# One-hot rows of a token behind one another, by twelve narrow compares per tile in place of three wide interleaved operations

## The reference, cut to what matters

```python
xn = _layernorm(x, axis=-1)
s = _L0_attn_ref(xn, ...)
g = _silu(_L0_ffn_ref(xn, ...))
x = x + s * g
# in _L0_ffn_ref: six of 32 experts for each token
idx, w = _route(xf, Wr, br)
gate = jnp.zeros((T, E), w.dtype).at[jnp.arange(T)[:, None], idx].add(w)
h = jnp.square(jax.nn.relu(xf @ w1.T)) @ w2.T      # per expert, acc += g * h
```

## Time and profile before

| | us |
|---|---|
| time, median of 3 runs | 384.15 |
| lowest and highest | 383.17, 384.49 |
| span of the profiled execution, first to last instruction | 381.1 |
| busy: TensorE, VectorE, ScalarE, GpSimd | 308.8, 269.4, 240.6, 221.0 |

### The profile page before, as it was taken

The page is one execution under the profiler, slowest core; times in us unless marked ns, Lnnn a source line. Parts: engine busy times, 40 slices in busy tenths (PEclk is TensorE's granted clock), DMA queues, the critical chain, the costliest instruction groups (busy, mean ns, idle before and its releaser), DMA issues.

```text
span 381.1 us, 8188 instructions
## 1 busy us (share of the span) xinstructions
PE 308.8 (81%) x2716; PEld 234.7 (62%) x2716; DVE 269.4 (71%) x634; ACT 240.6 (63%) x383; POOL 221.0 (58%) x232
## 2 busy tenths in 40 slices
PE   0585886899996878789798888789797798799962
PEld 0353654667785757677575676676475477687841
DVE  4688889998955286647567564447855786699866
ACT  5878799555484676676686576796645653544432
POOL 1966889855877356454663646500076565666750
PEclk9998699899999899999999999999999899899997
DMA  7951160254773366364644646434597565567742
GB/s 262 400 177 58 21 214 24 87 169 137 241 253 101 95 171 206 113 193 126 193 140 132 205 131 211 143 113 136 180 320 223 151 181 150 174 168 207 204 110 83
DMA packets 38762, 62.89 MB, mean 165 GB/s; under 512 B 5026, under 2 KB 26690, under 8 KB 38722
## 3 DMA queue, kind: packets, MB, share of 16 engines
q1 hardware_dynamic: 31474, 42.57, 34.4%
q0 software_dynamic: 7248, 19.80, 18.2%
HBM read 46.66 MB, written 15.70 MB: 164 GB/s over the span
## 4 chain that ended last, share of the span: by engine, by line
PE 52%; DVE 16%; issue 9%; ACT 9%; DVEq 6%; another core or an unknown queue 3%; POOL 2%; ACTq 2%; DMA 1%
PE hp L947 5%; PE hp L945 4%; PE hp L946 4%; PE rot L909 4%; PE hp L932 4%; PE dp L1001 4%; PE dp L1004 4%; PE dp L1003 4%; DVE xs L1284 3%; DVEq L1286 3%; PE hp L934 3%; PE bp L892 3%; DVE hf L1260 2%; PE rot L960 2%
## 5 line engine op out<-in xcount | busy, mean ns | idle before, releaser
L607 POOL DMA_INDIRECT xgt<-xtab,ids x91 | 93.7, 1029 | 63.7 <-PE rot L909 36.3
L617 POOL DMA_INDIRECT wst<-ytab,slot x60 | 62.7, 1045 | 61.3 <-DMA ytab<-wst 27.1
L688 ACT ACTIVATE hf<-hf 128x512 f32<-128x512 f32 (+1 forms) x80 | 49.9, 623 | 72.1 <-DVE hf L1260 52.8
L1001 PE MATMUL dp<-wt,hhi 128*128 128x256 f16 x204 | 56.7, 278 | 5.2 <-ACT xs L722 2.9
L1277 DVE COPY wst<-rot 128x512 f32<-128x512 f32 (+1 forms) x35 | 23.7, 680 | 51.7 <-PE rot L962 37.9
L1004 PE MATMUL dp<-wt,hhi 128*128 128x256 f16 x204 | 56.6, 277 | 1.2 <-issue 1.2
L1003 PE MATMUL dp<-wt,hlo 128*128 128x256 f16 x204 | 56.6, 278 | 1.0 <-issue 1.0
L693 ACT ACTIVATE hhi<-hf 128x512 f16<-128x512 f32 (+1 forms) x80 | 49.9, 624 | 5.7
L945 PE MATMUL hp<-xh,wt 128*128 128x512 f16 (+1 forms) x148 | 51.1, 345 | 0.9 <-DVE hf L1260 0.6
L703 ACT ACTIVATE xgt<-rot 128x1024 f16<-128x1024 f16 (+1 forms) x46 | 46.1, 1002 | 7.8 <-remote 5.0
L947 PE MATMUL hp<-xh,wt 128*128 128x512 f16 (+1 forms) x148 | 50.9, 344 | 0.0
(11 more groups left out here) (174 smaller groups left out, 703.1 us busy)
## 6 DMA issues: line engine op xcount, KB each, us to landing
gate_bc<-gtab SPq DMA_DIRECT2D x48, 256.0 KB
ytab<-wst SPq DMA_DIRECT2D x45, 256.0 KB
wst<-in_wts SPq DMA_DIRECT2D x17, 512.0 KB, 5.6
xs<-in_x SPq DMA_DIRECT2D x4, 512.0 KB, 5.0
xgt<-in_x SPq DMA_DIRECT2D x4, 512.0 KB
out<-xgt SPq DMA_DIRECT2D x16, 128.0 KB
xtab<-xn SPq DMA_DIRECT2D x3, 512.0 KB, 3.1
xgt<-xtab,ids POOLq DMA_INDIRECT x91
```

The costliest lines, as they stand in the source:

```text
L607: nc.gpsimd.indirect_dma_start(xg[:, a % XRING, :, :].rearrange("p h d -> p (h d)"), None, xtab, bass.IndirectOffsetOnAxis(ids[:, a:a + 1] ...
L617: nc.gpsimd.indirect_dma_start(yk[:, n % KRING, :], None, ytab, bass.IndirectOffsetOnAxis(slot[:, n // K, n % K:n % K + 1], 0))\
L688: nc.scalar.activation(hf[:, k % HP, 0:width(k)], hf[:, k % HP, 0:width(k)], ACT.Square, scale=W_SCALE ** (-0.5 if gated else -1.0))
L1001: nc.tensor.matmul(o, hhi[:, k % HRING, hcols], hi, start=(e == 0 and q % 2 == 0), stop=False, skip_group_check=True)
```

## The change

The rows of the one-hot arrays are laid out with the expert choice k outside and the 128 positions inside, where before the six choices of a position were neighbours. So the operands of `place` are contiguous. `one_hot` no longer makes them by two compares of 128x768 and one multiply of 128x768 with a drain ahead of it, but by twelve TENSOR_SCALARs of 128x128: six compare the iota with the scalar `fa` of the token and multiply by its number, six compare it with `fb`. The iota copy is 128x128 in place of 128x768, `fa` and `fb` are f32 in place of f16.

```diff
--- before.py
+++ after.py
@@ -132,7 +132,7 @@
         id16 = sb("id16", [P, P], F16)
         tri16 = sb("tri16", [P, P], F16)
         incl16 = sb("incl16", [E, E], F16)
-        iota6 = sb("iota6", [P, P, K], F16)
+        iota16 = sb("iota16", [P, P], F16)
         ones16 = sb("ones16", [P, P], F16)
         wr_sb = sb("wr_sb", [P, KC, E])
         wrhi = sb("wrhi", [P, KC, E], F16)
@@ -193,8 +193,8 @@
         slot = sb("slot", [P, NR, K], I32)
         slot_a = sb("slot_a", [P, NR, K], I32)
         slot_b = sb("slot_b", [P, NR, K], I32)
-        fa = sb("fa", [P, NR, K], F16)
-        fb = sb("fb", [P, NR, K], F16)
+        fa = sb("fa", [P, NR, K])
+        fb = sb("fb", [P, NR, K])
         ids = sb("ids", [P, P], I32)
         eq = sb("eq", [P, 2, K, E])
         root = eq[:, 0, 0:J, :]
@@ -204,7 +204,7 @@
         xgt = sb("xgt", [P, (XRING + TRING) * 2 * D], F16)
         xg = xgt[:, 0:XRING * 2 * D].rearrange("p (a h d) -> p a h d", h=2, d=D)
         xt = xgt[:, XRING * 2 * D:(XRING + TRING) * 2 * D].rearrange("p (a h r) -> p a h r", h=2 * KC, r=P)
-        hots = xgt[:, 0:2 * OHRING * P * K].rearrange("p (w s r k) -> p w s r k", w=2, k=K, r=P)
+        hots = xgt[:, 0:2 * OHRING * P * K].rearrange("p (w s k r) -> p w s k r", w=2, k=K, r=P)
         wq_sb = xgt[:, 2 * OHRING * P * K:2 * OHRING * P * K + 2 * KC * D].bitcast(F32).rearrange("p (k d) -> p k d", d=D)
         spare = xgt[:, 2 * OHRING * P * K + 2 * KC * D:2 * OHRING * P * K + 2 * KC * D + 2 * P].bitcast(F32)
 
@@ -738,7 +738,7 @@
             nc.scalar.activation(wrhi[:, :, :], wr_sb[:, :, :], ACT.Copy, scale=WR_SCALE).then_inc(consts_ready, 1)
             nc.scalar.activation(tri16[:, :], cst[:, P:2 * P], ACT.Copy)
             nc.scalar.activation(incl16[:, :], cst[0:E, 3 * P + NT:3 * P + NT + E], ACT.Copy)
-            nc.scalar.activation(iota6[:, :, :], iota.unsqueeze(2).broadcast_to([P, P, K]), ACT.Copy).then_inc(consts_ready, 1)
+            nc.scalar.activation(iota16[:, :], iota, ACT.Copy).then_inc(consts_ready, 1)
             def early(k):
                 relu(k)
                 act.drain()
@@ -889,7 +889,7 @@
                 for i in tiles:
                     pe.wait_ge(one_ready, i + 1)
                     for k in range(K):
-                        mm = nc.tensor.matmul(flat_q[:, 0:P], one_b[:, i % OHRING, :, k], one_a[:, i % OHRING, :, k],
+                        mm = nc.tensor.matmul(flat_q[:, 0:P], one_b[:, i % OHRING, k, :], one_a[:, i % OHRING, k, :],
                                               start=(i == 0 and k == 0), stop=(i == NR - 1 and k == K - 1),
                                               skip_group_check=True)
                     mm.then_inc(one_used, 1)
@@ -1299,13 +1299,12 @@
                 if i >= OHRING:
                     dve.wait_ge(one_used, i - OHRING + 1)
                 s = i % OHRING
-                nc.vector.tensor_tensor(one_a[:, s], iota6[:, :, :], fa[:, i, :].unsqueeze(1).broadcast_to([P, P, K]),
-                                        ALU.is_equal)
-                nc.vector.tensor_tensor(one_b[:, s], iota6[:, :, :], fb[:, i, :].unsqueeze(1).broadcast_to([P, P, K]),
-                                        ALU.is_equal)
-                dve.drain()
-                nc.vector.tensor_scalar(one_a[:, s], one_a[:, s], row_id[:, ROUTED[i]:ROUTED[i] + 1], None, ALU.mult)\
-                  .then_inc(one_ready, 1)
+                for k in range(K):
+                    nc.vector.tensor_scalar(one_a[:, s, k, :], iota16[:, :], fa[:, i, k:k + 1],
+                                            row_id[:, ROUTED[i]:ROUTED[i] + 1], ALU.is_equal, ALU.mult)
+                for k in range(K):
+                    op = nc.vector.tensor_scalar(one_b[:, s, k, :], iota16[:, :], fb[:, i, k:k + 1], None, ALU.is_equal)
+                op.then_inc(one_ready, 1)
 
             spread(0)
             shifts(0)
```

## The result

The changed kernel takes 391.78 us (median of 5 runs, 391.43 to 395.73) against 383.53 us before (median of 5): 8.25 us more, ratio 1.024, 95% interval 1.020 to 1.028. It is slower; the interval excludes no change, with its lower end at 2%. The forecast was 392.2.

A forecast was written before the change was run, and what follows sets the result against it. The prediction took the end of the one-hot loop, where VectorE and TensorE are both close, to pass any delay on. +7.8 compares, +1.0 contention, -1.2 placing and +0.5 clock made +8.1 on 384.15: 392.2 us, range 381 to 396.5.

The forecast's parts named there:

- What bounds: End of the one-hot loop: a delay there goes through VectorE and TensorE into everything behind, with no reserve.
- third rival: Stages behind the loop take up VectorE's delay, leaving a third of it: 384 to 388 us; chance 0.07.
- The compares: VectorE's twelve narrow compares per tile: 2.2 us against 1.43, 7.8 us more over ten tiles.
- the upper bound that I had named: One_a compares on VectorE: the second scalar costs another 0.056, a step 0.223 us, +9.2 over ten tiles.
- Contention: VectorE in the one-hot loop: small GpSimd operations may each stop it for 0.1 us; +1 us, from 0 to +1.5.
- The end of the placing: TensorE after tile 9 is ready: placing needs 0.4 us instead of 1.6, -1.2 us.
- The clock: TensorE behind the loop: waits lower the granted clock, costing 0 to 1.5 us, taken as 0.5.
- my bound: Upper end of the clock's cost on TensorE behind the loop: 1.5 us.
- Sum: Whole kernel: compares, contention, end of placing and clock together add 8.1 us, giving 392.2 us.
- The 3.05 us that I added between span and time: Whole kernel before: the median of the runs stands 3.05 us above the span of 381.1, giving 384.15.
- The rule: VectorE's compares by the skill page: 0.094 us each, a tile 1.13, the sum about 381 us.

The follow-up runs named there:

- third group: The last of three groups of experiments, each on another chip; its chip had the kernel before at 349.55 us.
- the control: The changed kernel with ids from a constant column instead of the placing matmuls' sum; ratio to the kernel before 1.024 (1.009 to 1.039), repeated 1.024 (1.020 to 1.027).
- runs with none, one and two scalars: The control with constants in all compares (ratio 1.000), with the row id left out of the first compare (1.019), and the control itself (1.024).
- run once more: The changed kernel without an edit, measured and profiled again; ratio to the kernel before 1.0255 (1.0105 to 1.0405).
- run with constants: The control with constants in the instruction for all scalars per partition of the compares; ratio to the kernel before 1.000 (0.995 to 1.005).
- strided ones: The control with placing matmuls reading every sixth element; ratio to the kernel before 1.022 (1.015 to 1.029), repeated 1.028 (1.024 to 1.032).
- wide compares with pairs: The new layout made by wide compares, with fa and fb holding each value twice; ratio to the kernel before 1.000 (0.996 to 1.004).

## Why the prediction was right

- *What bounds.* Right: the delay at the end of the loop went through whole. Last ReLU 9.2 us later, first routed unit 9.2, gathers 9.5 (101.11 against 91.61), time 8.25. In the third group, where the part behind the first routed unit takes 236 us instead of 274, the control's first routed unit stands at the same 120.86 us and it loses 8.9 us of 349.55 by the medians, 8.3 by the ratio: no part of the loss is seen to depend on what comes behind. The third rival (the stages behind take it up) is out.
- *The compares.* One scalar: 0.168 forecast, 0.162 measured. Two scalars: 0.20 forecast, 0.223 measured. The second costs what the first does, not half; that is the one term of the sum that was mis-sized by much, and the value is the upper bound that I had named. +8.8 us over ten tiles instead of +7.8. That the first fitted to 0.006 hides two small errors: the step without a scalar was 0.102, not 0.112, and the scalar 0.061, not 0.056. The price was inferred from rows behind a drain, and the runs with none, one and two scalars show that it is paid between neighbours too.
- *Contention.* +1.0 forecast; the loop from the first compare to the last ReLU is 35.6 us, 4 x 0.6 of other ReLUs and 23.1 of undisturbed tiles taken off leave 10.1; the same sum for the loop before (26.6 us, undisturbed tiles 14.3) gives 9.9. +0.2. Beside GpSimd's subtraction of 1.16 us at 93.29 six compares take 2.04 us (at 93.11) in place of 1.05: one stop for one GpSimd operation, as I had it, however many operations VectorE has. The small operations cost less than I gave them: beside them tile 3 (75.98 to 78.71) takes 0.4 us more than an undisturbed one. The loop before has seven of the subtractions, where I wrote ten; the sum went by the measured 9.5 us and does not change by it.
- *The end of the placing.* -1.2 forecast; from last ReLU to the first use of the sum 1.00 us (98.38 - 97.38) instead of 1.87, -0.9; in the run once more 0.68, -1.2.
- *The clock.* +0.5 forecast within 0 to 1.5, +1.2 measured on the first unit behind the loop (3.8 us instead of 2.6). In the two profiles of the control the unit took 4.3 and 4.0 us, so +1.4 to +1.7, partly above my bound.
- *Sum.* The loop started 0.2 later. 0.2 + 8.8 + 0.2 - 0.9 + 1.2 = +9.5 at the second unit behind the loop (101.94 against 92.4, that is 89.80 and one unit of 2.6 in the earlier trace rows), +9.2 at the first routed unit. The time's +8.25 against +8.1 is closer than the terms: the errors of the compares and of the clock were made good by the contention and by about 1 us behind the stage, which varies by more than that between executions. That part of the hit is luck. The 3.05 us that I added between span and time were 1.8 and, for the rest, a profiled execution that was faster than the median; it cancels in the difference.
- *The rule.* The Trainium skill, VectorE: DVE Perf Modes, section "The TRN2 errata", gives 58 cycles and the elements over the factor, an estimated 0.094 us for this compare. The run with constants shows 0.102, the wide compare 0.47, so the trace agrees for operations without scalars per partition; with them the rule falls short by 0.06 us each, and on 120 operations with 180 such scalars this is the difference between no change (the run with constants) and the loss. The 0.07 us by which the prediction found the multiply's row above the rule is also of the size of one such scalar.

## What to carry to other kernels

Before splitting a wide VectorE operation into narrow ones, count the scalars per partition as well as the operations: a 128x128 f16 compare had an estimated 0.034 us of streaming (from the prediction's rows) in a measured step of 0.10 to 0.22. The layout that suits TensorE can be had at the wide operations' full rate when the repeated operand is held in pairs. And work taken from TensorE was worth nothing measurable here while VectorE set its pace; it then ran in part at the lower clock and gave back what was left.

## What the runs showed of the hardware

- A scalar read per partition costs VectorE 0.06 us for each, in every one of neighbouring operations: 0.102, 0.163, 0.223 us a step.
- An f16 compare of two inputs over 128x768 takes 0.55 us with an innermost pair of neighbours in its second input, as with six neighbours, and 0.95 with an innermost repeat of one element.
- Under the same narrow compares, TensorE with the contiguous placing matmuls had the lower granted clock: 0.76 and 0.81 in the loop against 0.86 and 0.86 with strided ones. It is no rule: under the wide compares with pairs the contiguous ones had 1.00.
- One chip ran everything behind the first routed unit in 236 us that others ran in 274, with the stage up to it equal to 0.1 us (120.83 and 120.86). The waits of the changed kernel's profile between 120 and 340 us (engine, line, waited for: us in total, times, longest) name one source that it can't resolve. The kernel before has it too (23.0 us, 14 times, between 111 and 330 us), and it is not among the longest in the control's profile on the faster chip:

```profile
ACT hf L683 <- remote: 26.5, 15, 3.0
```

  What it is stays open.
